# Quantised blocks stored with the element index outside and the block index inside

## The reference

```python
def mx_quant(x):                       # BLOCK = 32, BITS = 8
    xb = x.reshape(s[:-1] + (s[-1] // BLOCK, BLOCK))
    amax = jnp.max(jnp.abs(xb), axis=-1, keepdims=True)
    shared_exp = jnp.floor(jnp.log2(jnp.where(amax > 0, amax, 1.0)))
    scale = jnp.exp2(shared_exp - (BITS - 2))
    q = jnp.clip(jnp.round(xb / scale), -2.0 ** (BITS - 1), 2.0 ** (BITS - 1) - 1) * scale

h = mx_layernorm(x, ln_w, ln_b)        # 128 x 512 a sequence
h = mx_linear(h, W1, b1)               # 512 -> 2048
h = mx_gelu(h)
h = mx_linear(h, W2, b2)               # 2048 -> 512
return bf16_round(residual + h)
```

## Time and profile before

| | |
|---|---|
| median of three runs | 1310.47 us |
| the profiled execution, its own time | 1312.03 us |
| its span, first to last instruction | 1310.2 us |
| PE busy | 1237.2 us (94%) |
| VectorE busy | 1150.3 us (88%), 1912 instructions |
| ACT busy | 814.9 us (62%) |
| GpSimd busy | 658.2 us (50%) |
| mean granted TensorE clock | 0.984 |

### The profile page before, as it was taken

How to read it: one execution, slowest core, us unless ns; L and a number is a source line. 1 busy time by engine, 2 the same in 40 slices (tenths; PEclk the granted TensorE clock), 3 DMA queues, 4 the chain that set the end, 5 groups by cost and what they waited for, 6 DMA issues and landing times.

```text
span 1310.2 us, 34536 instructions
## 1 busy us (share of the span) xinstructions
PE 1237.2 (94%) x13352; PEld 796.2 (61%) x13352; DVE 1150.3 (88%) x1912; ACT 814.9 (62%) x1581; POOL 658.2 (50%) x701
## 2 busy tenths in 40 slices
PE   5889999999999999999999999999999999999864
PEld 4657566666766666676666666766666666566421
DVE  8878889989989889988888998989888898899786
ACT  5355767665666676666667666666666665675541
POOL 8766355555464444555454455454435554454232
PEclk9989999999999999999999999999999999999987
DMA  9674222122223222223133223322222122221222
GB/s 271 188 168 106 54 64 71 41 56 79 55 76 80 55 51 55 73 69 70 47 85 49 57 54 73 77 64 65 62 57 58 56 68 66 72 56 35 69 61 52
DMA packets 137330, 97.08 MB, mean 74 GB/s; under 512 B 108112, under 2 KB 110160, under 8 KB 136400
## 3 DMA queue, kind: packets, MB, share of 16 engines
q1 hardware_dynamic: 137168, 94.87, 28.9%
HBM read 37.16 MB, written 8.39 MB: 35 GB/s over the span
## 4 chain that ended last, share of the span: by engine, by line
PE 73%; DVE 10%; issue 5%; POOL 5%; DMA 4%; ACT 2%; SPq 1%; POOLq 0%; ACTq 0%; DVEq 0%
PE bank_b L741 14%; PE bank_y L795 7%; PE bank_y L859 7%; PE bank_a L741 7%; PE bank_a L731 6%; PE rt L810 5%; PE rt L823 4%; PE rt L760 4%; PE bank_o L829 4%; PE bank_b L850 4%; PE bank_a L850 3%; PE bank_o L787 2%; DVE negm L1993 2%; PE bank_y L779 2%; DMA gmem<-w 2%
## 5 line engine op out<-in xcount | busy, mean ns | idle before, releaser
L4961 POOL TENSOR_TENSOR gmem<-gmem,unit_g 128x1024 bf16<-128x1024 bf16 x64 | 125.2, 1957 | 213.2 <-DVE unit_g L2046 213.2
L1993 DVE TENSOR_REDUCE negm<-rt 128x16 f32<-128x2048 f32 x64 | 146.2, 2284 | 11.7 <-PE rt L810 11.3
L3688 ACT ACTIVATE pT<-rt 128x2048 f32<-128x2048 f32 x64 | 120.0, 1875 | 42.1 <-PE rt L823 27.6
L741 PE MATMUL bank_a<-mix_r,w_Wr 128*128 128x128 f32 x1024 | 123.4, 279 | 3.1 <-POOL mix_r L4920 3.1
L859 PE MATMUL bank_y<-w2q,gmem 128*128 128x512 bf16 x512 | 119.6, 383 | 5.5 <-DMA gmem<-gmem 5.5
L741 PEld LDWEIGHTS bank_a<-mix_r,w_Wr 128*128 128x128 f32 x1024 | 118.7, 194 | 10.0 <-issue 9.0
L741 PEld LDWEIGHTS bank_b<-mix_k,w_Wk 128*128 128x128 f32 x1024 | 118.6, 193 | 6.0 <-issue 6.0
L741 PE MATMUL bank_b<-mix_k,w_Wk 128*128 128x128 f32 x1024 | 119.8, 275 | 2.1 <-DVE mix_k L1941 2.0
L741 PE MATMUL bank_b<-mix_g,w_Wg 128*128 128x128 f32 x1024 | 121.4, 277 | 0.0
L795 PE MATMUL bank_y<-w_Wo,yT 128*128 128x512 f32 x256 | 117.8, 603 | 3.8 <-DVE yT L1980 3.8
L731 PE MATMUL bank_a<-w_Wv,mix_v 128*128 128x512 f32 x256 | 117.3, 601 | 2.3 <-ACT rT L3614 2.2
(11 more groups left out here) (263 smaller groups left out, 2892.0 us busy)
## 6 DMA issues: line engine op xcount, KB each, us to landing
qx<-qdense SPq DMA_DIRECT2D x64, 224.0 KB, 3.4
context<-ctx SPq DMA_DIRECT2D x32, 384.0 KB, 3.6
xin<-x SPq DMA_DIRECT2D x32, 256.0 KB, 3.3
gmem<-w SPq DMA_DIRECT2D x16, 512.0 KB, 4.6
out<-x SPq DMA_DIRECT2D x32, 256.0 KB, 2.3
vp<-vz SPq DMA_DIRECT2D x32, 128.0 KB, 2.9
odense<-oT SPq DMA_DIRECT2D x128, 32.0 KB, 2.0
pT<-Wv SPq DMA_DIRECT2D x1, 1024.0 KB, 9.0
```

The source lines that it names most:

```text
L741: done = e.matmul(bank[:, m * T:(m + 1) * T], wt[f"W{name}"][:, c, m * P:(m + 1) * P], mix[name][:, c, :], start=(c == 0), stop=(c == KT - 1))
L1993: e.tensor_reduce(negm[:, 0:H].rearrange("p (g a j) -> p g j a", g=4, a=2)[:, :, 2 * i:2 * i + 2, :], rt[:, :].rearrange("p (g j a s) -> p ...
L3688: e.activation(pT[:, :, :].rearrange("p g n -> p (g n)"), rt[:, :], ACT.Exp, scale=float(D) ** -0.5).then_inc(sem(f"act_ex{i}"), 1)
L4961: e.tensor_tensor(blocks(half), blocks(half), per_block(unit[f"g{i}"], 32), ALU.mult).then_inc(sem(f"pool_gsc{i}"), 1)
```

## The change

A row of quantised blocks is now stored as (element, block): the first elements of all blocks, then the second ones. The host permutes the rows of W1 and b1 and the columns of W1 and W2 to match, so that ACT writes the GELU row in the new order without doing anything else; `hidden` on VectorE reads in the old order and writes in the new one, two bytes every 32. A maximum over a block now reads with a step of one row of blocks: 32 bytes in the hidden row, 64 in the GELU row, 128 in the weights.

Behind each row lies one more element per block that holds the least allowed value, and the maximum is taken over 33 elements; the instruction at L2039 goes, for all three kinds of row. The constants 0.25 at the end of both matmuls become 2^-20.

Rounding is now done by writing 16-bit integers. `gelu_round` multiplies by 32, takes the minimum with 127 and writes int16. The hidden row gets a step of its own for this, `hidden_round`, between `hidden_scale` and `hidden_quantised`; it stands in each of the 32 places of the order of VectorE. The last multiplication by the power of two is a plain `tensor_tensor` of int16 and bf16 into bf16. All other orders stay.

For the weights ACT writes 8-bit integers into the upper bytes of 16-bit elements whose lower bytes are zero. These lie no longer in the staging half but in `x2[2]` and in a new tile `zo` (which also holds what `z_bf` and `o_bf` held). So `load_w12` waits for ACT's `w12_rounded` and no longer for `w12_quantise`, and `w12_rounded(n)` waits for `w12_quantise(n - 2)`. GpSimd has two new lots of memsets: at its start, ahead of `pool_zeros` (two of 128 x 32 and two of 128 x 512 words), and `floors`, between `w12_scaled(15)` and `mixed(3, "g")`, which puts the least values behind the hidden row and the two GELU rows. `floors` waits for all pieces to be rounded and for the DMA transpose of piece 14; `hidden_max(0)`, the first `gelu_max` and ACT's first GELU wait for `floors`.

```diff
-        hz = sb("hz", [P, 2 * C], BF16)
+        hz = sb("hz", [P, 2 * C + C // BLK], BF16)
+        h_bf, h_all, z_even = hz[:, 0:C], hz[:, 0:C + C // BLK], hz[:, C + C // BLK:]
+        zo = sb("zo", [P, 2 * C], BF16)
-        w_int = [w[:, 0:FF // 8].bitcast(I8) for w in wst]
+        w_int = [t[:, :].bitcast(I16) for t in (x2[2], zo)]
-        def blocks(ap):
-            return ap.rearrange("p (b k) -> p b k", k=BLK)
+        def steps(ap, nb):
+            return ap.rearrange("p (k b) -> p k b", b=nb)
+        def blocks(ap, nb):
+            return ap.rearrange("p (k b) -> p b k", b=nb)
         def per_block(ap, nb):
-            return ap[:, 0:nb].unsqueeze(2).to_broadcast([P, nb, BLK])
+            return ap[:, 0:nb].unsqueeze(1).to_broadcast([P, BLK, nb])
...
             def load_w12(n):
                 if n >= 2:
-                    e.wait_ge(sem("dve_w_q"), n - 1)
+                    e.wait_ge(sem("act_w_int"), n - 1)
...
-                e.scalar_tensor_tensor(h_bf, hw[:, :], rstd["g"][:, 0:1], row["ffn_ln_b"][:, :],
-                                       ALU.mult, ALU.add).then_inc(sem("dve_hchain"), 1)
+                by_block = "p (b k) -> p b k"
+                e.scalar_tensor_tensor(blocks(h_bf, 16), hw[:, :].rearrange(by_block, b=16), rstd["g"][:, 0:1],
+                                       row["ffn_ln_b"][:, :].rearrange(by_block, b=16), ALU.mult,
+                                       ALU.add).then_inc(sem("dve_hchain"), 1)
-            def block_max(key, src, after, n, name):
+            def block_max(key, src, nb, after, n, name):
                 e.wait_ge(sem(after), n)
-                e.tensor_reduce(amax[key][:, :], blocks(src), AX_X, ALU.max,
+                e.tensor_reduce(amax[key][:, 0:nb], blocks(src, nb), AX_X, ALU.max,
                                 apply_absolute_value=True).then_inc(sem(name), 1)
-            def block_floor(key, name, n, steps):
-                e.wait_ge(sem(name), n)
-                e.tensor_scalar(upper(amax[key][:, :]), upper(amax[key][:, :]), LEAST_HALF + steps, steps,
-                                ALU.max, ALU.subtract).then_inc(sem(name), 1)
+            def to_steps(half):
+                return e.tensor_scalar(half.bitcast(I16), half, STEPS, MOST, ALU.mult, ALU.min)
             def hidden_scale(n):
-                e.tensor_tensor(blocks(h_int), blocks(h_bf), per_block(unit["h"], 16),
+                e.tensor_tensor(steps(h_bf, 16), steps(h_bf, 16), per_block(unit["h"], 16),
                                 ALU.mult).then_inc(sem("dve_hchain"), 1)
+            def hidden_round(n):
+                to_steps(h_bf).then_inc(sem("dve_hchain"), 1)
             def hidden_quantised(n):
-                e.tensor_tensor(blocks(h_bf), blocks(h_int), per_block(pow2["h"], 16),
+                e.tensor_tensor(steps(h_bf, 16), steps(h_bf.bitcast(I16), 16), per_block(pow2["h"], 16),
                                 ALU.mult).then_inc(sem("dve_hq"), 1)
             def gelu_round(n, i):
-                e.tensor_scalar(half.bitcast(FP16), half, TOP, MAGIC16, ALU.min, ALU.add).then_inc(sem(f"dve_gchain{i}"), 1)
+                to_steps(g_bf[i]).then_inc(sem(f"dve_gchain{i}"), 1)
             def gelu_quantised(n, i):
-                e.scalar_tensor_tensor(blocks(half), blocks(half.bitcast(FP16)), MAGIC16, per_block(pow2[f"g{i}"], 32),
-                                       ALU.subtract, ALU.mult).then_inc(sem(f"dve_gq{i}"), 1)
+                e.tensor_tensor(steps(g_bf[i], 32), steps(g_bf[i].bitcast(I16), 32), per_block(pow2[f"g{i}"], 32),
+                                ALU.mult).then_inc(sem(f"dve_gq{i}"), 1)
             def w12_quantise(n):
-                e.tensor_tensor(blocks(wq[n % 2]), blocks(w_int[n % 2]), per_block(pow2[key], 32),
-                                ALU.mult).then_inc(sem("dve_w_q"), 1)
+                e.tensor_tensor(pieces_out(n), pieces_in(n, steps(w_int[n % 2], 32)),
+                                pieces_in(n, per_block(pow2[f"g{n % 2}"], 32)), ALU.mult).then_inc(sem("dve_w_q"), 1)
...
             def w12_rounded(n):
                 e.wait_ge(sem("pool_w_scale"), n + 1)
-                e.activation(w_int[n % 2], wst[n % 2], ACT.Copy).then_inc(sem("act_w_int"), 1)
+                if n >= 2:
+                    e.wait_ge(sem("dve_w_q"), n - 1)
+                e.activation(w_int[n % 2].bitcast(I8)[:, 1::2], wst[n % 2], ACT.Copy,
+                             scale=STEPS).then_inc(sem("act_w_int"), 1)
...
             def gelu_scale(n, i):
-                e.tensor_tensor(blocks(half), blocks(half), per_block(unit[f"g{i}"], 32),
+                e.tensor_tensor(steps(g_bf[i], 32), steps(g_bf[i], 32), per_block(unit[f"g{i}"], 32),
                                 ALU.mult).then_inc(sem(f"pool_gsc{i}"), 1)
             def w12_scaled(n):
-                w = blocks(wst[n % 2])
+                w = steps(wst[n % 2], 32)
+            def floors():
+                e.wait_ge(sem("act_w_int"), PIECES)
+                e.wait_ge(sem("sp_wT0"), turned(14))
+                e.memset(h_all[:, C:], LEAST)
+                for g in g_all:
+                    done = e.memset(g[:, FH:], LEAST)
+                done.then_inc(sem("pool_floors"), 1)
...
             w12_scaled(15)
+            floors()
             mixed(3, "g")
             gate_rstd(2)
             with_bias(3)
```

More of the change, by code:

```diff
@@ L9 @@
 BF16 = mybir.dt.bfloat16
-FP16 = mybir.dt.float16
+I16 = mybir.dt.int16
 U16 = mybir.dt.uint16
@@ L2249, in _ @@
             hidden_scale(0)
+            hidden_round(0)
             hidden_quantised(0)
@@ L2331, in _ @@
             hidden_scale(2)
+            hidden_round(2)
             hidden_quantised(2)
@@ L2373, in _ @@
             hidden_scale(3)
+            hidden_round(3)
             norm_mv("q", 7)
@@ L2415, in _ @@
             hidden_scale(4)
+            hidden_round(4)
             hidden_quantised(4)
@@ L2584, in _ @@
             hidden_scale(8)
+            hidden_round(8)
             gelu_max(7, 1)
@@ L3322, in _ @@
             hidden_scale(25)
+            hidden_round(25)
             stats_x(27)
@@ L3362, in _ @@
             hidden_scale(26)
+            hidden_round(26)
             gated_y(28)
```

122 lines of the change are left out of this document (79 added, 43 removed).

## The result

The changed kernel took 1383.49 us (median; 1379.53 to 1388.18), the kernel before 1310.55 beside it: 1.0556 times as long, 95% interval 1.052 to 1.0592. That is 73 us slower, where 4 us faster was forecast. The profiled execution took 1385.05 us, with a span of 1383.2.

A forecast was written before the change was run, and what follows sets the result against it. PE was taken to bound the middle, so faster VectorE work could gain only at the two ends: -5 (start) + 3 (`floors`) - 2.3 (end) = -4.3 us, giving 1306.2 us from 1310.47, range 1302 to 1332.

The forecast's parts named there:

- Int16 pairs: Last multiplication of a GELU half on VectorE: 16-bit operands go in pairs, 1226 ns becomes 692; chance of no pairs 0.08.
- the hidden steps: `hidden_scale` and `hidden_quantised` on VectorE: 692 ns each become 418 each, -0.55 us together.
- GpSimd's scaling: `gelu_scale` and `w12_scaled` on GpSimd read a dense row: 2.14 us taken, +0.24 us an instruction.
- the end: From 1250 us on, savings in VectorE's steps less slower GpSimd scalings: -2.3 us, bounds -1 and -3.5.
- -5 + 3 = -2: First 140 us: about -5 us from a shorter chain (bounds 0 and -9), +3 us from PE's stall behind `floors`.
- PE's stall at `floors`: Near 130 us, `floors` holds up GpSimd's gate work: PE stalls 2.1 to 4.2 us, taken as +3.
- undisturbed pace: `mixed` on GpSimd behind `floors`: about 2.6 us without waits for the port, against 4.7 before.
- the lower end: VectorE's maxima: a step costs nothing, 1.03 ns per element; upper end half that rate, 2.33 us per GELU maximum.
- 752 + 512 x 1.03 = 1.28 us: Upper value for `hidden` on VectorE writing with a step of 32 bytes; 752 ns was taken.
- half rate with a step: Rival, chance 0.30: stepped access on VectorE runs at half rate, making it slower than before; 1321 us, 1313 to 1345.
- 3.8 us of idle time: VectorE's idle time per item of 36.7 us, read as room for some tenths of a us more work in the middle.
- the gain of the start: First 140 us: about -5 us from a shorter chain, PE idling near 24 us in the first 120.

The follow-up runs named there:

- all-dense kernel: The changed kernel with the `hidden` write and all maxima made dense, the rest of the change in place: 1306.08 us, 0.9971 of the kernel before.
- useless work of its size inside the same chain: The changed kernel with dense write and maxima, plus a useless 1677 ns VectorE reduction per item ahead of `hidden_scale`: 1325.28 us, 1.0103 of the kernel before.
- the maxima alone: The changed kernel with the `hidden` write made dense and the maxima still stepped: 1330.99 us, 1.0155 of the kernel before.

## Why the forecast failed

The sum of the parts: right wherever a row of the kernel before showed the same kind of instruction. Int16 pairs 693 ns for 692 forecast, which also bears out the rule of the Trainium skill (Vector Engine (DVE) Microarchitecture Reference, section 5.1) that of the types asks only for 2 bytes each; the hidden steps 426 for 418; `hidden_round` 294 for 300; GpSimd's scaling 2126 for 2140. With both steps dense the kernel takes 1306.08 us. By its trace the end fits: 74.1 us from the last output projection to the end, before 76.7, -2.6 where -2.3 stood in the sum. At the third item it is 2.4 us ahead of the kernel before, where -5 + 3 = -2 was said. That the pieces agree to tenths is partly luck: the two traces differ by 7.7 us in all, 2.7 of them in the middle where nothing was forecast, and the medians by 3.9. PE's stall at `floors` was 1.32 us in the changed kernel, not 2.1 to 4.2: `mix_g` and its product took 1.41 + 1.18 us there, which is the forecast's undisturbed pace of about 2.6 us and not the old 4.7; and `floors` was over at 132.5 us, not at 134.7.

**First step that failed: the price of a step.** "I take the lower end, because the reduction costs the same per element as two-input operations that fetch twice as much". That dense reductions and dense two-input operations cost the same per element says nothing of elements that are 32 bytes apart, and no row with neighbours could. The maxima came out between the two ends (1934 ns, ends 1250 and 2330): (1934 - 160) / 1056 = 1.68 ns per element, with the reduction's fixed 160 ns taken from 1212 - 1024 x 1.03. That is near the 1.73 ns per column that the Trainium skill (Vector Engine (DVE) Microarchitecture Reference, section 5.2) gives for one source that hops 4 KiB at every element, and not near its 2.50 for small steps. The write came out beyond my upper end: 2436 ns, where "752 + 512 x 1.03 = 1.28 us" was the bound; it is (2436 - 225) / 512 = 4.3 ns per element, with 752 - 512 x 1.03 = 225 fixed. The same section's 2.50 ns per column for 4-byte words written with a step would not have covered it: an estimate by it is 1.5 us. The bound was made by analogy to reads; for a 16-bit write there was nothing in the trace to make one from.

**Second step that failed, and the larger one: what VectorE's time is worth.** The rival "half rate with a step" had the work nearly right: 3.25 us per item more for stepping, measured 2 x 0.72 + 0.42 + 1.68 = 3.5. And yet it gave 1321 us, 1345 at most, against 1383.49. What failed is "So the middle bears a VectorE that gets some tenths of a us slower per item", read from 3.8 us of idle time, and, in the rival, an item that is slower by "+1.5 us, out of 3.8 idle", with the middle "taken as 4 us (0 to 20)". The runs showed in its place that this idle time is no slack: 1.7 us per item of stepped write put into the kernel before, less than half of the 3.8 idle, left VectorE's share at 89.6% and cost 71.3 us. That is 71.3 / 54 = 1.3 us for each us of stepped write, and 71.3 / 66.9 = 1.07 for each by which VectorE's busy time grew. With these prices, known only now, a range for the rival would have read 1310 + 32 x 1.5 x 1.1 to 1.3 = 1363 to 1372 us. (The forecast's item of 36.7 us is a mean over the ends too; in the middle it is 37.8, with 3.9 us idle, which changes nothing here.)

**What hid it.** PE idled 5.6 us in 1000. I took this as proof that PE alone was the bound. But PE's share says only that less work on VectorE gains nothing; it doesn't say how much more VectorE can take. The run without the stepping shows the other side: 40 us less of VectorE's work from 200 to 1200 us gave 1 us in the middle (604.7 and 603.7 us for 16 items), so a faster VectorE bought nothing, as forecast. The mistake was to read this one-sided fact as a two-sided one.

PE's idle time in the first 120 us was 27.2 us, before 28.7, not 24, also in the all-dense kernel (27.1): the gain of the start doesn't show as idle time of PE in that stretch. What stays open: why the stepped write costs 13.6 us more than useless work of its size inside the same chain, of which its effect on GpSimd can be only a part; why the maxima alone, which bring VectorE to the same work per item as before (33.8 us, at 37.9 per item), lose 20 us against the kernel before, 12.4 of them by the tenth item.

## What to carry to other kernels

Where an engine's list is in a fixed order and its neighbours wait for it in turn, a busy share near 90% can be all that it has: don't price added work there at zero out of its idle time (here it cost from 0.2 to 1.3 us per us, by its amount and its place), and ask which bound comes second. Before a layout is changed, measure one instruction of the new kind by itself, in the same form; here 19 of them behind the last step gave the prices of the steps in one run. When a layout has to serve a reduction along one axis and a paired operation along another, an innermost run of two elements was enough for the pairs and kept every step at 4 bytes.

## What the hardware showed

- Reductions of VectorE that read 512 bf16 elements with a step: 686 ns up to 8 bytes, 1005 to 1066 ns at 16 bytes and more.
- `scalar_tensor_tensor` of two f32 sources, 512 elements written with a step: in bf16 786 ns at 4 bytes, 1356 at 8, 2361 to 2483 from 16 on (752 dense); in f32 1123 at 16 and 1080 at 64. A one-source `tensor_scalar` from bf16 to bf16 took 1236 at 32 bytes.
- Beside that bf16 write with a step of 32 bytes GpSimd's instructions take longer: GpSimd is busy 672.2 us in place of 660.6 in the whole all-dense kernel, and 672.7 in place of 658.2 in the kernel before. A useless one-source reduction of the same excess didn't do this (658.1).
- An innermost run of two 16-bit elements keeps the fast rate of 16-bit multiplications (693 ns for 1024, as with a dense run of 32), and a row repeated with such a run is read by GpSimd as cheaply as one element repeated (1901 ns), against 2126 for a dense row of 32.
- A pause of PE of 3.10 us was followed by a granted clock of 0.79 and 1.66 us of slower matmuls; another, of 3.53 us, was followed by a clock of 1.00.
